# Attention scores as 32-row products of four heads at once, with other PSUM banks and one step for rest and sums

## The reference

```python
x = x + xattn(layernorm(x), ctx)          # x: 4096 x 512, ctx: 3202 x 512, 16 heads of 32
#   q = layernorm(x) @ Wq + bq ; k = ctx @ Wk + bk ; v = ctx @ Wv + bv
#   A = softmax(q k^T / sqrt(32)) over the 3202 keys ; out = (A v) @ Wo + bo
x = x + ffn(layernorm(x))                 # 8 experts of 512 x 512, the two best per token,
#   weighted by their share of the router's softmax over all 8
```

## Time and profile before

| | us |
|---|---|
| median of 3 runs | 2495.17 (2495.07 to 2497.3) |
| the profiled execution's own time | 2496.92 |
| its span, first to last instruction | 2494.8 |
| TensorE matmul busy | 2418.3 (97%) |
| VectorE busy | 2154.4 (86%) |
| ScalarE busy | 1841.8 (74%) |
| GpSimd busy | 400.4 (16%) |

### The profile page before, as it was taken

One profiled execution on the slowest core, in us unless ns is written; L12 is line 12 of the kernel. 1 busy time (PEld: TensorE's weight loads), 2 busy tenths in 40 slices (PEclk: granted clock), 3 DMA queues, 4 the chain that ended last, 5 costly groups with the idle time before them and its releaser, 6 DMA issues. The chain is left out here.

```text
span 2494.8 us, 36973 instructions
## 1 busy us (share of the span) xinstructions
PE 2418.3 (97%) x13522; PEld 1284.4 (51%) x13522; DVE 2154.4 (86%) x1941; ACT 1841.8 (74%) x2157; POOL 400.4 (16%) x512
## 2 busy tenths in 40 slices
PE   8999699999999999999999999999999999969998
PEld 7878444444444444444444444444444447758776
DVE  4368499999999999999999999999999998867555
ACT  3123399989889989898998989898899876624333
POOL 2113210100000000000000000000000003236654
PEclk9999799999999999999999999999999999979999
DMA  7436690111150011115101111500101017644463
GB/s 267 162 124 227 193 215 23 27 27 26 35 124 23 23 27 27 30 31 125 23 23 27 27 33 28 125 23 22 30 24 35 18 60 254 224 114 142 139 210 121
DMA packets 131352, 214.12 MB, mean 86 GB/s; under 512 B 26822, under 2 KB 64166, under 8 KB 130412
## 3 DMA queue, kind: packets, MB, share of 16 engines
q1 hardware_dynamic: 104268, 144.67, 20.7%
q0 software_dynamic: 24576, 59.52, 7.7%
q10 hardware_dynamic: 2336, 7.60, 0.9%
HBM read 146.36 MB, written 83.04 MB: 92 GB/s over the span
## 5 line engine op out<-in xcount | busy, mean ns | idle before, releaser
L1124 ACT ACTIVATE probs<-psum 128x1024 f32<-128x1024 f32 x1600 | 1509.0, 1035 | 148.2 <-PE psum L1275 144.2
L1275 PE MATMUL psum<-q_st,k_st 97*128 97x512 f32 x3200 | 921.7, 419 | 15.6 <-DVE k_st L943 12.3
L1275 PEld LDWEIGHTS psum<-q_st,k_st 97*128 97x128 f32 x3200 | 547.7, 188 | 592.3 <-ACT probs L1124 413.4
L1187 DVE TENSOR_TENSOR even_sums<-even_sums,probs 128x2048 f32<-128x2048 f32 x352 | 806.4, 2291 | 0.2 <-ACT probs L1124 0.2
L1296 PE MATMUL psum<-probs,v_st 128*32 128x512 f32 x6400 | 799.1, 601 | 0.0
L1187 DVE TENSOR_TENSOR odd_sums<-odd_sums,probs 128x2048 f32<-128x2048 f32 x320 | 732.1, 2288 | 1.0
L1296 PEld LDWEIGHTS psum<-probs,v_st 128*32 128x32 f32 x6400 | 152.2, 108 | 352.0 <-issue 263.9
L2056 PE MATMUL psum<-we_hi,wo 128*128 x624 | 219.3, 413 | 7.7 <-ACT wo L1895 5.2
L800 POOL DMA_DIRECT2D sum_scratch<-shared_rows x31 | 18.3, 590 | 1207.6 <-ACT shared_rows L1079 1207.6
L2056 PEld LDWEIGHTS psum<-we_hi,wo 128*128 128x128 f32 x624 | 119.8, 192 | 34.5 <-issue 8.8
L1888 ACT ACTIVATE shared_rows<-hold 128x512 f32<-128x512 f32 x78 | 63.5, 814 | 84.0 <-DMA hold<-token_rows,whole 46.0
(11 more groups left out here) (230 smaller groups left out, 2050.8 us busy)
## 6 DMA issues: line engine op xcount, KB each, us to landing
q_st<-qh_scratch SPq DMA_DIRECT2D x64, 256.0 KB
k_st<-kh_scratch SPq DMA_DIRECT2D x56, 192.0 KB, 3.7
token_rows<-rows SPq DMA_DIRECT2D x8, 1028.0 KB, 6.7
xn<-in_x SPq DMA_DIRECT2D x16, 512.0 KB, 6.5
qh_scratch<-o_hi SPq DMA_DIRECT2D x8, 1024.0 KB, 4.5
ql_scratch<-o_lo SPq DMA_DIRECT2D x8, 1024.0 KB, 7.6
q_st<-ql_scratch SPq DMA_DIRECT2D x32, 256.0 KB
token_rows<-in_x SPq DMA_DIRECT2D x1, 8192.0 KB, 37.3
```

Of the source, the lines that this page charges most:

```text
L1124: nc.scalar.activation(probs[:, p_slot(it, t), 2 * half:2 * half + 2, :], psum[:, 2 * slot:2 * slot + 2, :], ACT.Exp, scale=SCALE).then_in ...
L1187: nc.vector.tensor_tensor(into[:], a, probs[:, p_slot(it, t)], ALU.add).then_inc(added, 1)
L1275: mm = nc.tensor.matmul(psum[:, 2 * slot + h % 2, :], k_st[:, h, t * P:(t + 1) * P], q_st[b][:, h, :], start=True, stop=True)
```

## The change

- `k_st` and `q_st` hold high and low parts side by side, the four heads on 32 partitions each. A tile's scores are three rounds (`TERMS`) of four products of 32 rows, head h on partitions 32h to 32h + 31, each into a bank of its own.
- The bound is no row any more. `neg_bound` is a column of 128 x 1 that every exponential takes as its bias. The way of the bound through HBM goes. The branch for inputs whose scores have too wide a bound keeps a shift row, as a fourth round; it is the other arm of an If on SP and TensorE, and for this input it isn't taken.
- PSUM: bank 7 for the first head of every tile, banks 0 to 2 and 3 to 5 in turn for the other three heads, bank 6 for the attended values. A tile has two exponentials, one of 512 and one of 1536 columns. TensorE computes scores two tiles ahead (`AHEAD_TILES`); each tile's scores wait for the first head's exponential of the tile before (`first_done`).
- At tile 4 (`REST_TILE`) come the rest's products (three of 128 rows), its exponential and split, then the sums of the previous iteration in one go (`sum_probs`: rest, tile 24 directly, odd, even), and their copy. VectorE adds one tile less (22 additions). `odd_sums` has two buffers, `probs` 9 tiles.
- Keys and queries come in two transfers each instead of three and four. The last 2 keys of all groups are loaded once. The rows of ones are no longer filled; VectorE fills `shift_ones`, `rest_shift` and the shift part of both `q_st` instead.

```diff
 HG = P // DH
 WIDEST = 30.0
 SLACK = 1.02
-S_RING = 3
-P_RING = 8
-FETCH_AT = 6
-ODD_SUMS_AT, EVEN_SUMS_AT = 0, 3
-REST_PAIR = 36
-REST_KEYS_AT = 9
-REST_LOW_AT = 17
-SUMS_COPY_AT, INVERT_AT, NORMALISE_AT = 16, 9, 13
+P_RING = 9
+FIRST_BANK, SETS, ATTENDED_BANK = 7, (0, 3), 6
+REST_TILE = 4
+DIRECT_TILE = 24
+REST_LOW_AT, REST_V_AT, REST_AT = 8, 18, 21
+INVERT_AT, NORMALISE_AT = 6, 11
 WO_AFTER, REST_AFTER = 3, 5
-FIRST_HIGH_AT, FIRST_LOW_AT = 40, 21
-LEAD = 7
+FETCH_TILE = 1
+WO_TILE, REST_V_TILE, BO_TILE = 8, 16, 8
+FIRST_HIGH_TILE, FIRST_LOW_AT = 20, 20
+AHEAD_TILES = 2
+SHIFT_PART = 2
+TERMS = ((0, 0), (0, 1), (1, 0))
...
@@ -332,11 +328,6 @@
                 sp.wait_ge(q_stored[0], 32)
                 load_queries(sp, g, 0, 0, g["q_in"][0])
-                sp.wait_ge(neg_rows_ready, 1)
-                sp.dma_start(shift_d.rearrange("g j (c n) -> (g j c) n", n=CH), neg_rows.bitcast(F32)).then_inc(shift_stored, 16)
-
-                sp.wait_ge(shift_stored, 16)
...
-                pe.matmul(psum[:, Q_SUM_BANK, :], ones_row[:], neg_bound[:], start=True, stop=True).then_inc(neg_spread, 1)
+                pe.matmul(psum[:, K_SUM_BANK, 0:P], norms[:].to_broadcast([P, P]), ident[:], start=True, stop=True).then_inc(norms_turned, 1)
...
-    for r, src in enumerate((g["qh_d"], g["ql_d"], g["qh_d"])):
-        sp.dma_start(g["q_st"][b][r * DH:(r + 1) * DH, :, :].bitcast(F32),
-                     src.rearrange("(h d) j l -> d h (j l)", d=DH)[:, :, ds(it * CH, CH)]).then_inc(count, 16)
+    for part, src in enumerate((g["qh_d"], g["ql_d"])):
+        sp.dma_start(g["q_st"][b][:, part, :].bitcast(F32), src.rearrange("p j l -> p (j l)")[:, ds(it * CH, CH)]).then_inc(count, 16)
...
+        k_st = sb("k_st", [P, 2, S], F32R)
+        q_st = g["q_st"]
+        shift_ones = sb("shift_ones", [P, P], F32R)
...
-            for r, src in enumerate((kh_d, kh_d, kl_d)):
-                sp.dma_start(k_st[r * DH:(r + 1) * DH, :, first:first + n].bitcast(F32),
-                             src[:, ds(j, 1), first:first + n].rearrange("(h d) o s -> d (h o) s", d=DH)).then_inc(count, 16)
-        adds = NT - 2
-        last_odd_add = adds - 1 - NT % 2
+            for part, src in enumerate((kh_d, kl_d)):
+                sp.dma_start(k_st[:, part:part + 1, first:first + n].bitcast(F32), src[:, ds(j, 1), first:first + n]).then_inc(count, 16)
+
...
+        def place(t):
+
+            return t + (t >= REST_TILE)
+
+        def bank(t, h):
+
+            return SETS[place(t) % 2] + h - 1 if h else FIRST_BANK
+
+        REST_BANK = SETS[REST_TILE % 2]
+        SUM_BANK = REST_BANK + 1
+        adds = NT - 3
...
                 def copy_sums(it):
                     act.wait_ge(sums_ready, it + 1)
-                    if not (isinstance(it, int) and it == 0):
+                    if it > 0:
                         act.wait_ge(o_final, it)
                     act.activation(recip, psum[:, SUM_BANK, :], ACT.Copy).then_inc(sums_copied, 1)
+                def rest(it):
+
+                    act.wait_ge(s_ready, it * STEPS + REST_TILE + 1)
+                    if it > 0:
+                        act.wait_ge(rest_ready, it)
+                    act.activation(rest_probs[:], psum[0:REST_ROWS, REST_BANK, :], ACT.Exp, bias=neg_bound[0:REST_ROWS], scale=SCALE).then_inc(exp_done, 1)
+                    act.wait_ge(exp_done, it * STEPS + REST_TILE + 1)
+                    if it > 0:
+                        act.wait_ge(rest_used, it)
+                    act.activation(rest_split[:], rest_probs[:], ACT.Copy).then_inc(rest_high, 1)
...
+                            act.wait_ge(pv_done, was * NT + u + 1)
+                            if u == DIRECT_TILE:
+                                act.wait_ge(sums_ready, was + 1)
+                            else:
                                 act.wait_ge(added, was * adds + add_of(u) + 1)
-                        nc.scalar.activation(probs[:, p_slot(it, t), 2 * half:2 * half + 2, :],
-                                             psum[:, 2 * slot:2 * slot + 2, :], ACT.Exp, scale=SCALE).then_inc(exp_done, 1)
+                        p = p_slot(it, t)
+                        act.activation(probs[:, p, 0, :], psum[:, FIRST_BANK, :], ACT.Exp, bias=neg_bound[:], scale=SCALE).then_inc(first_done, 1)
+                        if t == FETCH_TILE and it > 0:
+                            fetch(it - 1)
+                        act.activation(probs[:, p, 1:HG, :], psum[:, bank(t, 1):bank(t, 1) + HG - 1, :], ACT.Exp,
+                                       bias=neg_bound[:], scale=SCALE).then_inc(exp_done, 1)
...
+                dve.wait_ge(filled, 8)
+                for h in range(HG):
+                    dve.memset(rest_shift[h * DH:h * DH + 1, :].rearrange("p (o x) -> p o x", x=DH)[:, :, h * LAST:(h + 1) * LAST].bitcast(F32), 1.0).then_inc(filled, 1)
                 dve.wait_ge(filled, FILLS)
                 for o in (0, DH):
@@ -1167,20 +1165,24 @@
                         dve.tensor_scalar(neg[:], mxx[:], -1.0, None, ALU.mult).then_inc(ma_neg, 1)
...
-                    into = odd_sums if t % 2 else even_sums[it % 2]
-
-                    dve.wait_ge(exp_done, it * NP + place(t, 1) + 1)
+                    into = odd_sums[it % 2] if t % 2 else even_sums[it % 2]
+
+                    dve.wait_ge(exp_done, it * STEPS + place(t) + 1)
                     if k == 0 and it > 1:
                         dve.wait_ge(sums_ready, it - 1)
-                    if k == 1 and it > 0:
-                        dve.wait_ge(odd_summed, it)
...
-                            if it == 0:
-                                dve.wait_ge(rows_filled, K_PIECES)
-                                dve.wait_ge(filled, FILLS + K_PIECES)
-                            for o in (0, DH, 2 * DH):
-                                dve.tensor_copy(rest_places(o), k_st[:, :, S - LAST:S])
...
+                def products(it, t, h, term, start, stop):
+
+                    part, of = TERMS[term]
+                    rows = slice(h * DH, (h + 1) * DH)
+                    return nc.tensor.matmul(psum[:, bank(t, h), :], k_st[rows, part, t * P:(t + 1) * P], q_st[it % 2][rows, of, :], start=start, stop=stop)
+
+                def scores(it, t, shifted):
+
+                    if t == 0:
+
+                        pe.wait_ge(q_in[it % 2], queries_in(it, shifted))
+                    if t in piece_of:
+
+                        pe.wait_ge(k_in[piece_of[t] % 2], 32 * arrivals(it // NC, piece_of[t]))
+
+                    if t == REST_TILE:
+                        pe.wait_ge(exp_done, it * STEPS + REST_TILE)
+                    elif it * NT + t >= 1:
+                        pe.wait_ge(first_done, it * NT + t)
+                    for term in range(len(TERMS)):
+                        last = term == len(TERMS) - 1 and not shifted
+                        for h in range(HG):
+                            mm = products(it, t, h, term, term == 0, last)
+                    if shifted:
+                        for h in range(HG):
+                            row = slice(h * DH, h * DH + 1)
+                            mm = nc.tensor.matmul(psum[:, bank(t, h), :], shift_ones[row, :], q_st[it % 2][row, SHIFT_PART, :], start=False, stop=True)
+                    mm.then_inc(s_ready, 1)
+
+                def rest_scores(it, shifted):
+
+                    b, j = it % 2, it // NC
+                    pe.wait_ge(exp_done, it * STEPS + REST_TILE - 1)
+                    if it == 0:
+                        pe.wait_ge(rest_k_built, HG)
+                    for term, (part, of) in enumerate(TERMS):
+                        mm = nc.tensor.matmul(psum[0:REST_ROWS, REST_BANK, :], rest_k[:, j, part, 0:REST_ROWS], q_st[b][:, of, :],
+                                              start=term == 0, stop=term == len(TERMS) - 1 and not shifted)
+                    if shifted:
+                        mm = nc.tensor.matmul(psum[0:REST_ROWS, REST_BANK, :], rest_shift[:, 0:REST_ROWS], q_st[b][:, SHIFT_PART, :], start=False, stop=True)
+                    mm.then_inc(s_ready, 1)
+
+                def weigh_rest(it):
+                    pe.wait_ge(rest_ready, it + 1)
...
+                def sum_probs(it, bank):
+
+                    nc.tensor.matmul(psum[:, bank, :], rest_ones[:], rest_split[:], start=True, stop=False).then_inc(rest_used, 1)
+                    over_keys(bank, lambda h: ones[:], lambda h: probs[:, p_slot(it, DIRECT_TILE), h, :], False, False)
+                    pe.wait_ge(added, (it + 1) * adds)
+                    over_keys(bank, lambda h: ones[:], lambda h: odd_sums[it % 2][:, h, :], False, False)
+                    over_keys(bank, lambda h: ones[:], lambda h: even_sums[it % 2][:, h, :], False, True).then_inc(sums_ready, 1)
+
+                def ahead(it, t, shifted):
+
+                    if t >= NT:
+                        it, t = it + 1, t - NT
+                    if it < NIT:
+                        if t == REST_TILE:
```

(49 more changed lines are left out.)

374 lines of the change are left out of this document (163 added, 211 removed).

## The result

The kernel after takes 2505.18 us (median of 6 runs, 2503.08 to 2507.18); the kernel before took 2495.12 us beside it. The ratio is 1.0034, 95% interval 1.0024 to 1.0045: slower by 0.34%, where 2478 us and faster was forecast. The time lies in the range of 2430 to 2550 and outside the forecast's own 2466 to 2500; the direction was wrong. The profiled execution has a span of 2505.3 us, 10.5 more than before. It is the slowest of the six, 2.0 above their median, as the profiled one before was 1.8 above its own.

A forecast was written before the change was run, and what follows sets the result against it. TensorE was taken to bound the kernel, VectorE close behind. Start -5.7, first two iterations +1.5, 30 x (53.85 - 54.46) and end +4.7 gave -17.8 us, hence 2478 us; range 2430 to 2550.

The forecast's parts named there:

- Scores: Score products of a tile on TensorE: three packed rounds at 0.233 us, 0.91 a tile, 1.91 with the values.
- wider rounds: Score rounds wider than one product through weight loads: up to 0.30 us a round, 2490 to 2545 us, chance 0.14.
- no packing: The twelve score products run 0.233 us apart, 4.0 us a tile, above 4000 us in all; chance 0.06.
- The bound: Engine that sets the pace after the change: ScalarE at 1.985 us a tile, with TensorE at 1.91.
- 22 x 1.985: ScalarE from tile 4's first exponential to the next iteration's tile 1: 22 tiles at 1.985 us, 43.67 us.
- the slot chain stays shorter: First head's exponential, then next scores, back to ScalarE: 1.74 us, less than ScalarE's 1.985 a tile.
- Tile 1: ScalarE at tile 1: first head 0.57, wait 0.19, copy of attended values 0.49, three heads 1.415; 2.66 us.
- Tile 2 to tile 4: Path through TensorE's scores, values, rest products and sums until tile 4's exponentials can start: 7.49 us.
- VectorE: VectorE loses one addition of 2.20 us; 50.0 us of work and a chain of 50.7 stay hidden under 53.85.
- Start: Before the first score product: attention begins 4.7 us sooner without the bound's way, fills give 1.0 more; -5.7 us.
- First two iterations: Splits of Wo, rest values and bias lie on ScalarE, now the bound: +1.5 us, bounds 0 and 2.8.
- End: After the last fetch VectorE's later additions delay the projection and sums: 61.9 us against 57.2, so +4.7.

## Why the prediction was wrong

**Scores, right.** A round of four at 0.233 us, a tile's scores at 0.91, TensorE at 1.91 a tile: measured 0.90 and 1.90. In the records of the kernel after four products start within 0.01 us of each other, and three such rounds 0.34 and 0.23 apart; single 97-row products in a burst start 0.33 and then 0.23 to 0.24 apart in the kernel before. The rivals of wider rounds and of no packing fell with that. The estimate of 0.304 for a round, worked out from the Trainium skill (TensorE: Matmul & The Clock Gate, Measured speedup vs the span model), is not borne out: 0.23.

**The bound, right.** ScalarE takes over from TensorE. One round of scores and the constant bias show it from both sides.

**The step that failed is the term "22 x 1.985"** in the walk round the iteration, and with it "the slot chain stays shorter". It made 43.67 us; the 22 tiles took 54.52 - 2.79 - 7.45 = 44.28 (from one first head's exponential to the next, means of iterations 5 to 27). Two mistakes in it: from start to start a tile is 1.994, since the column costs 0.0925 and not 0.085; and TensorE is released by ends, which are 0.016 further apart; where the lengths reach 0.85, the slot chain, put at 1.74, takes 2.01. Both give 22 x 0.025 = 0.55 of the 0.61; the last 0.06 is what the iteration lost without the rest's value product. The run with one round of scores tells the two apart: there TensorE has room, the lengths grow as well, and the same 22 tiles take 43.84, so 0.17 is the column and 0.44 the two engines meeting. The column's price was taken from copies of 512 columns in rows 6. The Trainium skill (ScalarE: Activation LUTs, What ACT_TABLE_LOAD costs) has about 93 ns per pointer operand: from start to start the trace agrees with it within 1 ns.

**Tile 1** was put at 2.66 and took 2.79. The exponential before it is 0.69 long, as assumed, but tile 1 begins a piece of keys, so its scores start 0.14 after that exponential's end (1011.91 to 1012.05) and not 0.05. The last values, which stand behind them, are late by that 0.09, and the copy waits 0.30 and not 0.19. With one round of scores, where that chain is short, it is 2.66; without the rest's value product, where the exponential is 0.85 long, it is 2.93.

**Tile 2 to tile 4**: 7.49 forecast, 7.45 measured, and the two sums left out confirm that it is on the path. The rest's value product costs TensorE 0.43 from its start to the next product's (1006.75 to 1007.18 in the trace of after), where the walk has no term for it; by the run without it, it is worth 0.06 an iteration.

The margin was 54.46 - 53.85 = 0.61 us, 1% of an iteration, times 30. My own range for the forecast allowed for a bias of up to 0.09 and for 0.3 at the stop at tile 4, but for no other error in the term that counts 22 times. The chance of faster, 0.58, was too high for a margin of that size on a term of that size. That the time still lies in the stated range is luck: it lies there because the range took in the wider rounds (2490 to 2545), which did not happen.

**VectorE** hidden: right. Its chain was put at 50.7; alone, with one round of scores, it measures 50.2, as it should with two rounds less in it.

**Start**: attention begins at 284.3, 5.4 sooner with 4.7 forecast. Then the first load of keys came 3.4 us behind it instead of about 1.0, and the first product at 292.2, 3.0 sooner with 5.7 forecast. The step said "1.0 for the barrier as now" and did not price the branch over an arm that now holds 32 iterations of its own. Without the arm the first product is at 287.2.

**First two iterations**: +1.5 forecast, +4.7 measured. The step counted ScalarE's splits but not who waits for the low part behind VectorE: 5.3 us at tile 23 of the first iteration. The whole stretch missed by 3.2, but its first tile alone takes 2.5 to 4.3 us in traces with the same code there, so it can't be split finer. The hole is my own sign of error ("a first iteration longer by more than 3 us").

**End**: the projection starts 55.74 after the thirty-first copy, 55.7 forecast. It was put at 3.2 us long and took 4.4 (2051.19 to 2055.59) behind the pause, 1.2 of the 1.9 that the end misses (+6.6 instead of +4.7); the run with the earlier split took 3.7 off it. Where the other 0.7 went wasn't looked for.

The misses are 20.6 us in the iterations, 3.2 in the first, 2.7 at the start and 1.9 at the end: together the 28.3 between -17.8 and +10.5 but for rounding.

## What to carry to other kernels

Price the operands of the engine that becomes the bound before its partner's gain is counted: here packing brought what it promised, and one pointer operand on two instructions a tile gave all of it back (64 us). Where two engines take turns through few slots, the room of one is not free, and a forecast gain of about 1% of a repeated term is little more than a forecast of no change, above all where the term's rate was read from starts alone: look at the ends too, since other engines are released by them. A change that makes one engine free also makes others late: look, in the first and last iteration, at each one-time step that stands behind the engine that now lags.

## What the runs showed of the hardware

- Row-wise packing: four products of 32 rows and 512 columns, with loads of 128 columns each, run side by side at the pace of one: four start within 0.01 us, twelve cover 0.97 us, with the rounds 0.34 and 0.23 apart, as single 97-row products are.
- ScalarE's instructions grow longer, by 0.016 to 0.025 us per tile of two exponentials, while it never pauses, up to 1.04 for an instruction of 0.68 (one round of scores), and fall back after the first pause; what waits for their ends is late by as much.
- The start of attention came 5 us later with the long untaken arm in the program than without it.
- After a pause of 3.47 us in the first iteration TensorE's granted clock was 0.50 from 351 to 354, after one of 2.34 us at the end from 2051 to 2054; eight records that take 1.06 us took 1.93 in the first of these.
- One 72-row product between groups of 128*32 tiles takes 0.43 us of TensorE, where products in a row start 0.23 apart.
